# A per-sequence matrix multiply: sequences sorted by their matrix, rows gathered by the next stage

## What is computed

```python
w = weight[adapter_ids]                  # 64 ids in 3..7, weight is (8, 512, 512)
y = jnp.einsum('bsi,boi->bso', x, w)     # _L0_cond_ref: one matrix for each sequence
x = x + _L0_ffn_ref(y, ...)              # up, relu squared, down, latent expert, layer norm
```

## Time and profile before

| | us |
|---|---|
| median of 3 runs | 3812.58 (3808.99 to 3816.25) |
| the profiled execution | 3816.99 |
| its span in the trace | 3815.2 |
| first stage, until its last matmul has ended | 193.1 |
| second stage's first product begins | 214.7 |
| second stage's last result, store issued | 502.6 |

### The profile page before, as it was taken

How to read it: one execution, slowest core, us unless ns; L and a number is a source line. 1 busy time by engine, 2 the same in 40 slices (tenths; PEclk the granted TensorE clock), 3 DMA queues, 4 the chain that set the end, 5 groups by cost and what they waited for, 6 DMA issues and landing times. The chain is left out here.

```text
span 3815.2 us, 70659 instructions
## 1 busy us (share of the span) xinstructions
PE 3511.6 (92%) x22968; PEld 3224.1 (85%) x22968; DVE 2442.6 (64%) x6597; ACT 1609.6 (42%) x3658; POOL 1491.9 (39%) x2474
## 2 busy tenths in 40 slices
PE   8979969996987999999679999989999998999789
PEld 6868859995875888888679999989999997888677
DVE  2134344333236899999788888888888885322542
ACT  3132222222222454544456666656666664322221
POOL 1011120001112688888655555555555551000111
PEclk9989989998988999999889999999999999999888
DMA  3131052223333555545566666656666666433421
GB/s 125 51 116 45 23 142 83 76 71 110 109 119 102 158 166 165 166 161 166 167 214 209 217 210 216 211 181 218 212 217 213 215 215 190 130 108 105 130 92 55
DMA packets 444775, 560.67 MB, mean 147 GB/s; under 512 B 170362, under 2 KB 330362, under 8 KB 428027
## 3 DMA queue, kind: packets, MB, share of 16 engines
q1 hardware_dynamic: 425978, 421.92, 35.9%
q0 software_dynamic: 18432, 134.23, 10.1%
HBM read 389.28 MB, written 166.72 MB: 146 GB/s over the span
## 5 line engine op out<-in xcount | busy, mean ns | idle before, releaser
L1779 POOL CAST l2a_K<-l2a_Kall 128x256 fp32r x1524 | 593.9, 439 | 430.0 <-issue 429.9
L183 PE MATMUL l2a_s<-l2a_K,l2a_Q 128*128 128x288 f32 (+1 forms) x3072 | 521.3, 306 | 52.9 <-DVE l2a_K L1937 45.4
L2048 PE MATMUL l2a_x<-l2a_pt,l2a_V 128*128 128x128 f32 x4096 | 544.0, 276 | 3.3 <-DVE l2a_pn L1989 3.2
L2048 PEld LDWEIGHTS l2a_x<-l2a_pt,l2a_V 128*128 128x128 f32 x4096 | 505.0, 194 | 3.8 <-issue 3.7
L183 PEld LDWEIGHTS l2a_s<-l2a_K,l2a_Q 128*128 128x128 f32 x3072 | 428.6, 192 | 54.1 <-issue 52.8
L1970 DVE CUSTOM_DVE_ANT_0 l2a_sm<-l2a_s,l2a_B 128x544 f32<-128x544 f32 x512 | 369.7, 722 | 92.4 <-PE l2a_s L183 80.3
L1919 ACT ACTIVATE l2a_p<-l2a_sm,l2a_st 128x544 f32<-128x544 f32 x512 | 379.5, 741 | 32.5 <-DVE l2a_st L1973 32.3
L1905 ACT ACTIVATE l2a_pt<-l2a_t 128x512 f32<-128x512 f32 x512 | 305.7, 597 | 128.2 <-PE l2a_t L2034 128.0
L2034 PE MATMUL l2a_t<-ident,l2a_p 128*128 128x128 f32 x2048 | 336.0, 287 | 5.4 <-ACT l2a_ao L1912 5.4
L1980 DVE TENSOR_SCALAR l2a_p<-l2a_p,l2a_st 128x512 f32<-128x512 f32 x512 | 285.4, 557 | 18.2
L2034 PEld LDWEIGHTS l2a_t<-ident,l2a_p 128*128 128x128 f32 x2048 | 288.0, 209 | 6.5 <-issue 5.9
(11 more groups left out here) (820 smaller groups left out, 9081.7 us busy)
## 6 DMA issues: line engine op xcount, KB each, us to landing
s_qT<-l2q_qo SPq DMA_DIRECT2D x128, 512.0 KB, 3.0
l2a_Q<-s_qT SPq DMA_DIRECT2D x128, 512.0 KB, 5.7
s_ao<-l2a_ao SPq DMA_DIRECT2D x64, 512.0 KB, 5.1
l2o_a<-s_ao SPq DMA_DIRECT2D x128, 256.0 KB, 3.0
s_kn<-l2q_ko SPq DMA_DIRECT2D x128, 128.0 KB, 3.1
l2a_kn<-s_kn SPq DMA_DIRECT2D x32, 512.0 KB, 6.0
l2q_stage<-in_wqkv SPq DMA_DIRECT2D x32, 384.0 KB, 4.1
s_act<-l1u_ac SPq DMA_DIRECT2D x88, 128.0 KB, 1.9
```

The costliest lines, as they stand in the source:

```text
L183: i = pe.matmul(out, a, b, start=start and m + z == 0, stop=stop and 3 * m + z == n - 1)
L1779: e.tensor_copy(K[:, j:j + 1, :, :].rearrange("p a z n -> p a (z n)"), Kall[:, bass.ds(v, 1), :, :].rearrange("p a z n -> p a (z n)")).the ...
L2048: pe.matmul(px[:, P:256], V[:, k * D + hg * P:k * D + hg * P + P], pt[:, k, :], start=k == 0, stop=False)
```

## The change

In the first stage the 64 sequences are sorted by their matrix. Each matrix gets as many groups of four lanes as it needs, at most 64/4 + 7 = 23 groups (92 lanes, of which 64 are in use), so that one group has one matrix and all 128 columns of the stationary operand are filled. A table (`src`: which sequence is in a lane, `mat`: which matrix a group has, `lanes`: where a token's row lies) is computed on the chip by DVE and three small matmuls. ACT and DVE fill a group's `xm` lane by lane, with the address in `xs` from a register. x and weights are loaded whole, without slots; low parts are made by DVE alone, evictions too. PE works on the first 8 groups block by block, first high x high and low x high, then, after all four blocks, high x low; the other 15 groups follow one at a time. The result is stored plainly, group by group, and `l0_ffn` gathers its rows with indirect DMAs on POOL by `lanes`. The loads of `wg` go to SP's queue in `l0_ffn`, behind the store of each token tile; `xr` gets a third buffer; the fourth weight tile is no longer behind row fetches. Left out below are declarations, the seven small loads (ids twice, iota, icol, m4, m16, pcol), the first DVE steps of the table and the semaphores that live longer than a stage (`gather_in`, `values_in`).

```diff
+    def gather(self, pool, t, rows):
+        if t >= self.nat.n:
+            pool.wait_ge(self.turned, t - self.nat.n + 1)
+        pool.indirect_dma_start(self.nat[t][:, :], None, self.src,
+                                bass.IndirectOffsetOnAxis(ap=rows[:, t:t + 1], axis=0)).then_inc(self.nat.sem(t), 16)
...
+    NG = NB // 4 + 7
+    NL = 4 * NG
+    W = st.pair("w", [P, 4, 8, D])
+    xs = st.sb("xs", [P, 4, 2048])
+    NX = 9
+    xm = [st.pair(f"xm{i}", [P, 4, P]) for i in range(NX)]
+    y = st.slots("y", 2, [P, D])
...
-    steps = [(half, k, g) for half in range(2) for k in range(4) for g in range(8)]
...
+            for k in range(4):
+                sp.dma_start(xs[:, k, :], A["xT"][k * P:(k + 1) * P, :]).then_inc(x_in[k], 16)
+            for q in range(16):
+                k, a = q // 4, 2 * (q % 4)
+                sp.dma_start(w_tile(W[1], q).bitcast(F32),
+                             A["w0t"][a:a + 2, k * P:(k + 1) * P, :].rearrange("a p n -> p a n")).then_inc(w_in[q], 16)
             sp.dma_start(ident[:, :], A["ident"]).then_inc(ident_in, 16)
-            sp.dma_start(subj[:, :], A["ids3"].rearrange("(a n) -> a n", a=1)).then_inc(subj_in, 16)
-            r = [sp.alloc_register(f"subj{m}") for m in range(4)]
-            for n, (half, k, g) in enumerate(steps):
-                if g == 0 and n < 56:
-                    x_chunk(n // 8 + 1)
-                if n == 30:
-                    sp.wait_ge(subj_in, 16)
-                if 30 <= n < 62 and n % 2:
-                    b = (n - 30) // 2
-                    sp.reg_load(r, subj[0:1, 4 * b:4 * b + 4])
-                    for j in range(4):
-                        v = sp.snap(r[j], min_val=0, max_val=31)
-                        sp.dma_start(wg[32 * j:32 * j + 32, b, :],
-                                     A["w3"][bass.ds(v, 1), :, :].rearrange("a p n -> (a p) n")).then_inc(wg_in, 16)
-                if k == 3:
-                    e = 8 * half + g
-                    sp.wait_ge(copied, e + 1)
-                    sp.dma_start(S["y0"][e * P:(e + 1) * P, :], y[e][:, :]).then_inc(y.sem(e), 16)
-        @block.gpsimd
-        def _(pool):
-            for hl in xm[1:]:
-                for z in hl:
-                    pool.memset(z[:, :, :].bitcast(F32), 0.0).then_inc(zero_g, 1)
-            for q in range(2, 32, 3):
-                w.low(pool, q)
+            for s in range(NG):
+                sp.wait_ge(copied, s + 1)
+                sp.dma_start(S["y0"][s * P:(s + 1) * P, :], y[s][:, :]).then_inc(y.sem(s), 16)
...
+            def high(s):
+                if s >= NG:
+                    return
+                if s >= NX:
+                    act.wait_ge(mm, s - NX + 1)
+                act.reg_load(r, src[0:1, 4 * s:4 * s + 4])
+                for j in range(4):
+                    v = act.snap(r[j], min_val=0, max_val=NB - 1)
+                    act.activation(lane(xm[s % NX][0], j), xs[:, :, bass.ds(v * 32, 32)], ACT.Copy).then_inc(x_hi, 1)
+            def weights(k):
+                for q in range(4 * k, 4 * k + 4):
+                    act.wait_ge(w_in[q], 16)
+                    act.activation(w_tile(W[0], q), w_tile(W[1], q).bitcast(F32), ACT.Copy).then_inc(w_hi, 1)
+            act.wait_ge(tabled, 1)
+            for k in range(4):
+                act.wait_ge(x_in[k], 16)
             high(0)
+            weights(0)
+            for s in range(1, 8):
+                high(s)
+            for k in range(1, 4):
+                weights(k)
+            for s in range(8, NG):
+                high(s)
...
+            def low(s):
+                if s >= NG:
+                    return
+                dve.reg_load(r, src[0:1, 4 * s:4 * s + 4])
+                for j in range(4):
+                    v = dve.snap(r[j], min_val=0, max_val=NB - 1)
+                    h, l = (lane(z, j) for z in xm[s % NX])
+                    dve.wait_ge(x_hi, 4 * s + j + 1)
+                    dve.tensor_tensor(l, xs[:, :, bass.ds(v * 32, 32)], h.bitcast(F32), ALU.subtract).then_inc(x_lo, 1)
+            def weights(k):
+                for q in range(4 * k, 4 * k + 4):
+                    dve.wait_ge(w_hi, q + 1)
+                    dve.tensor_tensor(w_tile(W[1], q), w_tile(W[1], q).bitcast(F32), w_tile(W[0], q).bitcast(F32), ALU.subtract).then_inc(w_lo, 1)
+            def evict(s):
+                dve.wait_ge(mm, s + 1)
+                if s >= 2:
+                    dve.wait_ge(*y.landed(s - 2))
+                dve.tensor_copy(y[s][:, :], banks[s % 8][:, :]).then_inc(copied, 1)
...
+            dve.wait_ge(tab_mm, 1)
+            dve.tensor_copy(src[:, :], banks[7][0:1, 0:NL]).then_inc(tabled, 1)
+            dve.reduce_max(mat[:, 0:NG], banks[7][0:1, P:P + NL].rearrange("p (s j) -> p s j", j=4), AX).then_inc(tabled, 1)
+            dve.wait_ge(pcol_in, 16)
+            dve.tensor_scalar(lanes[:, :], banks[7][:, 256:256 + NT], 32.0, pcol[:, 0:1], ALU.mult, ALU.add).then_inc(tabled, 1)
+            dve.wait_ge(tabled, 1)
+            for s in range(1, 8):
+                low(s)
+            for k in range(4):
+                weights(k)
+            low(8)
+            for s in range(NG):
+                evict(s)
+                low(s + NX)
...
+            pe.wait_ge(placed, 2)
+            pe.wait_ge(icol_in, 16)
+            pe.wait_ge(m16_in, 16)
+            pe.matmul(banks[7][:, 0:NL], icol[:, 0:1].broadcast_to([NB, P]), row[:, :], start=True, stop=True)
+            pe.matmul(banks[7][:, P:P + NL], val[:, 1:2].broadcast_to([NB, P]), row[:, :], start=True, stop=True)
+            pe.matmul(banks[7][:, 256:256 + NT], m4[:, :], m16[:, :], start=True, stop=True).then_inc(tab_mm, 1)
+            pe.wait_ge(tabled, 3)
+            def group(s, k, passes, first=False, last=False):
+                pe.reg_load(r, mat[0:1, s:s + 1])
+                at = pe.snap(r, min_val=0, max_val=7) * D + k * 8 * D
+                for m in passes:
+                    a, z = xm[s % NX][m == 1], W[m == 2]
+                    i = pe.matmul(banks[s % 8][:, :], a[:, k, :], z[:, :, :, :].rearrange("p k a n -> p (k a n)")[:, bass.ds(at, D)],
+                                  start=first and m == passes[0], stop=last and m == passes[-1])
+                return i
+            for k in range(4):
+                pe.wait_ge(w_hi, 4 * k + 4)
+                for s in range(8):
+                    if k == 0:
+                        pe.wait_ge(x_lo, 4 * s + 4)
+                    group(s, k, (0, 1), first=k == 0)
+            for k in range(4):
+                pe.wait_ge(w_lo, 4 * k + 4)
+                for s in range(8):
+                    i = group(s, k, (2,), last=k == 3)
+                    if k == 3:
+                        i.then_inc(mm, 1)
+            for s in range(8, NG):
+                pe.wait_ge(x_lo, 4 * s + 4)
+                pe.wait_ge(copied, s - 7)
+                for k in range(4):
+                    i = group(s, k, (0, 1, 2), first=k == 0, last=k == 3)
...
-            for k in range(13, 16):
-                sp.wait_ge(*before_y.landed(k))
-            for t in range(8):
-                front.fetch(sp, t)
             w.fetch(sp, 3)
+            sp.dma_start(subj[:, :], A["ids3"].rearrange("(a n) -> a n", a=1)).then_inc(subj_in, 16)
             sp.dma_start(gam[:, :], row_bc(A["gamma"], D)).then_inc(gam_in, 16)
             sp.dma_start(bet[:, :], row_bc(A["beta"], D)).then_inc(bet_in, 16)
-            for cb in range(4):
-                if cb == 0:
-                    for m in range(8):
-                        for k in extra(m):
-                            w.fetch(sp, k)
-                if cb < 2:
-                    for t in range(8 + 4 * cb, 12 + 4 * cb):
-                        front.fetch(sp, t)
-                for tt in range(4 * cb, 4 * cb + 4):
-                    if tt >= 2:
-                        sp.wait_ge(*xr.landed(tt - 2, 2))
+            def x_tile(tt):
+                if tt < NT:
+                    if tt >= 3:
+                        sp.wait_ge(*xr.landed(tt - 3, 2))
                     sp.dma_start(xr[tt][:, :], A["x"][tt * P:(tt + 1) * P, :]).then_inc(xr.sem(tt), 16)
-                    sp.wait_ge(done, tt + 1)
-                    sp.dma_start(S["x1"][tt * P:(tt + 1) * P, :], xr[tt][:, :]).then_inc(xr.sem(tt), 16)
+            for m in range(8):
+                for k in extra(m):
+                    w.fetch(sp, k)
+            x_tile(0)
+            x_tile(1)
+            sp.wait_ge(subj_in, 16)
+            r = [sp.alloc_register(f"subj{m}") for m in range(4)]
+            for tt in range(NT):
+                x_tile(tt + 2)
+                sp.wait_ge(done, tt + 1)
+                sp.dma_start(S["x1"][tt * P:(tt + 1) * P, :], xr[tt][:, :]).then_inc(xr.sem(tt), 16)
+                sp.reg_load(r, subj[0:1, 4 * tt:4 * tt + 4])
+                for j in range(4):
+                    v = sp.snap(r[j], min_val=0, max_val=31)
```

(14 more changed lines are left out.)

164 lines of the change are left out of this document (66 added, 98 removed).

## The result

The changed kernel takes 3718.85 us (3715.03 to 3721.82), the kernel before, measured beside it, 3810.78 (3807.92 to 3816.25): a ratio of 0.9757, 95% interval 0.974 to 0.9773. The forecast was 3727, so its direction and range hold and its point is 8 us high. The profiled execution took 3715.03, its span is 3713.2.

A forecast was written before the change was run, and what follows sets the result against it. The prediction took the first stage to be bound by PE's number of matmuls. First stage 83.1 us less, hand-over 6 less, next gap 3.5 more: 85.6 less, so 3812.6 - 85.6 = 3727 us, range 3712 to 3750.

The forecast's parts named there:

- Number of matmuls: First stage on PE: 276 matmuls instead of 768, by pace alone 111.7 us less.
- The front: First-stage start: x complete at 19 us, weights at 45, lanes 1.3 per group, high passes until 53.1.
- Rivals 2 and 5: First stage: slower loads or lanes at the front, 3743, chance 0.22; register-addressed lanes slower than before, over 3813, chance 0.02.
- The sequencer in the passes: First 8 groups on PE: 0.50 us per index load, so 4.0 us per block in high and low passes.
- rival 1: First-stage passes: the sequencer doesn't bind, PE runs at matmul pace; time 3714 with quick hand-over, chance 0.15.
- The 15 groups: Rest of the first stage: 12 matmuls each, 2.72 us per group, 40.8 us, sequencer just hidden at about 2.65.
- Hand-over: First to second stage: first matmul 15.5 us after the first stage's last, against 21.6 now; 6 us less.
- M: Time at which the first stage's last matmul ends: 193.1 before, forecast 110, so 83.1 us earlier.
- Rival 3: Hand-over: each of four gathers takes POOL 2.83 us instead of 0.96; time 3737, chance 0.11.
- Second to third stage: Gap before the third stage: w3 loads on SP's queue +2.4, 19 more semaphores +1.1, together 3.5 us more.
- Low parts on VectorE alone: First stage: slower DVE-only low parts ready at 55.7, last low-pass block at 65.1, so they cost nothing.
- The second stage: Second stage: its length of 288 us stays unchanged.

The follow-up runs named there:

- main_regs: Changed kernel with one index load instead of four for each of the last 15 groups; first stage's last matmul at 104.5, single execution 3706.31 us.
- low_with: Changed kernel with each block of the first 8 groups making its three matmuls together, low pass not last; single execution 3715.41 us.
- passes_regs: Changed kernel with the first 8 groups' indices loaded once into eight registers before the passes; single execution 3712.71 us.
- before_fetch3: Kernel before, with the second stage's fourth weight tile fetched after four row fetches instead of eight; single execution 3808.16 us.
- wg_first: Changed kernel with the w3 loads back in the first stage, ahead of the stores of y; single execution 3732.50 us.
- variant: Changed kernel with four edits: both register edits, last w3 loads moved earlier, fourth row tile after fourth weight tile; median 3710.27 us, ratio 0.9729 to kernel before.
- the repeat: Changed kernel once more, unedited; second stage 276.2 us, span 3720.1 us.

## Why the prediction was right, and where it was off

**Number of matmuls: right.** 276 big matmuls, and the 15 groups run at 2.72 us wherever the sequencer lets them (main_regs, low_with).

**The front: mis-sized, 6.1 us too late** (high passes ended at 46.9 to 47.0, forecast 53.1). x was issued at 5.21, not 3.9, as each of the seven small loads took near 0.6 of SP; but the transfer was faster than the 320 GB/s assumed, 363 with the DMA engines at a share of 0.99, and the lanes cheaper: ACT's groups of four follow each other every 0.80 us, the load of 0.31 within it, against 1.3. DVE needs 1.24 for a group. Block 1 started at 35.1 (forecast 39.9), which is 4.8 of the 6.1; the rest is the pace of the blocks, told next. Rivals 2 and 5 had the same terms on the wrong side. The lane's upper bound came from a load of 0.6 us for four indices on DVE in another stage; at the front DVE's loads took 0.34 to 0.37. From 61 to 80 us, though, most of them took 0.6 again (the rows under main_regs), where PE did not wait for them.

**The sequencer in the passes: right for the low pass, wrong for the high ones.** The sequencer needs 0.50 us per group, the chosen middle between the bounds 0.35 and 0.61, and the low pass took 16.4 us against 16.0; passes_regs shows the cause. But the prediction put the high passes at 4.0 us a block too, and they took 3.63, the matmuls' own pace, as its rival 1 had them: the loads had got ahead while PE followed the lanes and the half clock. The Trainium skill's page "DMA: Bandwidth & Descriptors", section "Latency and other measured facts", puts a tensor_load at about 600 ns at least; the trace has 0.30 as the median and 0.294 as the least, and the measurement decides.

**The 15 groups: 2.8 us too short.** They took 43.6 instead of 40.8. The step that failed: the sum took the sequencer at a fixed 2.65 per group as "just hidden" under 2.72. With loads of up to 0.587 it is not hidden, and main_regs gave 2.4 back. Two instruction streams within 3% of each other are no cover.

**Hand-over: half right.** The weight tile's part was right, and before_fetch3 shows it. The gathers were issued 1.25 to 1.41 us apart instead of 0.96 (there is 0.30 between them, and the first took 1.11), the first at M + 3.65, and the fourth took 7.2 us to land, not 5.0: it landed at M + 14.7 instead of M + 11. 7.2 is near the end of the stated range (3.4 to 7.4). The first took 5.5 and the third at most 5.4, so the discount for the smaller transfer was near right for these; the fourth weight tile was issued beside the fourth gather, but that it drew the landing out was not tested. Rival 3 (slow gathers beside DVE's work) did not happen: the longest took POOL 1.11. In the kernel before, too, 124 of the 128 gathers ran beside a copy from SBUF to SBUF on DVE, and those took 0.95 in the median.

**Second to third stage: right**, 3.6 against 3.5. wg_first and variant each take 2.4 to 2.8 of it back, the share given to SP's w3 loads; the rest, 1.1 for the semaphores, was not tested by itself.

**Low parts on VectorE alone: right that they cost nothing** (ready at 51.8, needed at 59 for the last block), but against sharing every third with POOL they earn 4.2 us, which the prediction did not see: it called them the slower way.

**The second stage: the step that failed** was "its length unchanged" (288 there, as it reached to the clearing of the semaphores). Work unchanged is right, time unchanged is not: 281.3 and 280.1 before, 270.9 and 276.2 after. The two profiled executions of the changed kernel give back 5 to 10 us of half clock. In the medians, 92 us apart, the first stage is worth 86 to 88.5, the hand-over 2 to 3 and the gap -3.6 to -3.9; 4 to 8 are left for the second stage and all that stands behind it, which whole times cannot separate. Without that the forecast would be off by little: -86.2 - 2.8 + 3.6 = -85.4, against -85.6. That agreement is partly luck, since +6.1 at the front and -2.8 in the groups and -3.3 in the hand-over cancel.

What the prediction lacked is the row that shows the kernel's clock in that stage: it fell four times in it before the change as well, each time in the gate product, so there was time at half clock that could come out longer or shorter. What stays open is what sets the moment of the fall within that product; with it the time at half clock goes from 27 to 51 us, and the repeat alone moved it by 13.

## What to carry to other kernels

Count the sequencer's work per matmul, not only the matmul: when sparse work leaves one matmul per register load, load the registers once ahead. Before a helper engine is added or kept, look in the trace whether the main engine's own instructions grow while it runs. And when the gain of an early stage is read from whole times, cut both profiles at the same events first, and hold each stage's length against its granted clock, since a clock spell can hand out or eat a tenth of the gain. Where the clock fell, look at what the engine did there, and not only at whether it was busy.

## What was unexpected of the hardware

- A subtraction of two SBUF tiles on GpSimd stretched VectorE's from 1.21 to 3.41 us, and GpSimd's own from 2.36 to 3.36; together they were no faster than VectorE alone.
- An index load on PE took 0.30 us in the median and up to 0.587, also 0.577 when neither ACT nor DVE loaded an index; what draws it out is not shown.
- The second stage, 256 to 258 us of work at full clock in every profile, spent 27 to 51 us at half clock. Four of its five spells began 2.2 to 5.5 us behind the first of 48 matmuls of 8 columns and lasted 3.4 to 13.7 us; ahead of the last three of them PE had been busy without a break.
